# A fused scan, attention and feed-forward kernel: the products of weight matrices move from the attention into the scan

## The reference, cut to what matters

```
x:(64,64,512) float32                                    # 64 sequences, 64 channels, 512 wide
u  = einsum('bct,bcd->bdt', x, weights[cond])            # 64x64 matrix per sequence
x_dbl = einsum('bld,ed->ble', u, x_proj_w)               # delta_r (128), B (16), C (16)
delta = softplus(einsum('blr,dr->bld', delta_r, dt_proj_w) + dt_proj_b)
h_t = exp(delta*A) * h_(t-1) + (delta*u)*B ;  y = sum_n h_t*C  (+ u*D)     # state 16 per channel
x1 = x + y
q,k,v = x1 @ Wq.T, x1 @ Wk.T, x1 @ Wv.T ; q,k = rope(rms(q)), rope(rms(k))
k,v are written into paged blocks (16 tokens a block) ; window 256, softmax, 8 heads on 4 key groups
o  = attention(q, k_all, v_all)                          # (64,64,512)
z  = einsum('bto,do->btd', o, Wo)
s  = einsum('bld,d->bl', z, w_r) ; idx = top_k(s, l/2)   # half of the tokens of a sequence
f  = gelu(z[idx] @ w1 + b1) @ w2 + b2                    # w1 512x2048, w2 2048x512
x_out = x1 + scatter(f, idx)
```

## Time and profile before

| profile of before | |
|---|---|
| median of 3 runs | 1906.06 us |
| the profiled execution | 1905.25 us, span 1903.6 us |
| PE busy | 1671.7 us (88%) |
| DVE busy | 1456.6 us (77%) |
| ACT busy | 1280.2 us (67%) |
| POOL busy | 1268.8 us (67%) |
| chain that ended last | PE 45%, ACT 3%, issue 1%, DMA 1%, DVE 1% |

### The profile page before, as it was taken

One profiled execution on the slowest core, in us unless ns is written; L12 is line 12 of the kernel. 1 busy time (PEld: TensorE's weight loads), 2 busy tenths in 40 slices (PEclk: granted clock), 3 DMA queues, 4 the chain that ended last, 5 costly groups with the idle time before them and its releaser, 6 DMA issues.

```text
span 1903.6 us, 30576 instructions
## 1 busy us (share of the span) xinstructions
PE 1671.7 (88%) x9567; PEld 1154.6 (61%) x9567; DVE 1456.6 (77%) x2572; ACT 1280.2 (67%) x4006; POOL 1268.8 (67%) x1255
## 2 busy tenths in 40 slices
PE   6687878887877787777799899999999999999998
PEld 5665556665665565555355575756657575665765
DVE  8999999999999999999456665655656565565522
ACT  5888888888888888866356664655647465564621
POOL 5789999999999999988777654544545544450000
PEclk9899999999999999888899999999999999999999
DMA  5423323332333223322777434334343443431011
GB/s 207 155 104 147 146 97 124 146 135 109 122 147 147 112 112 142 133 78 73 218 207 217 116 104 124 105 108 130 99 128 103 115 117 110 120 94 60 30 62 45
DMA packets 117745, 230.71 MB, mean 121 GB/s; under 512 B 31365, under 2 KB 70293, under 8 KB 112465
## 3 DMA queue, kind: packets, MB, share of 16 engines
q1 hardware_dynamic: 84496, 163.48, 24.2%
q0 software_dynamic: 33088, 65.28, 12.7%
HBM read 212.09 MB, written 44.70 MB: 135 GB/s over the span
## 4 chain that ended last, share of the span: by engine, by line
PE 45%; ACT 3%; issue 1%; DMA 1%; DVE 1%; POOL 0%; ACTq 0%; DVEq 0%; SPq 0%; POOLq 0%
PE attn_psum L2003 12%; PE attn_psum L2019 12%; PE attn_psum L1933 4%; PE attn_psum L1920 4%; PE attn_psum L1913 4%; PE attn_psum L1960 3%; PE attn_psum L1904 2%; PE attn_psum L2037 2%; PE attn_psum L1894 1%; PE attn_psum L1945 1%; ACT xh L1644 1%; ACT th L1645 1%; ACT prob L1601 0%; DMA kv_at<-kv_scratch,new_now 0%; ACT a_sb L1631 0%
## 5 line engine op out<-in xcount | busy, mean ns | idle before, releaser
L1051 DVE TENSOR_TENSOR_SCAN hid<-scan_psum,hid 128x1024 f32<-128x1024 f32 x256 | 581.1, 2270 | 0.0
L1240 PE MATMUL scan_psum<-ident,hid 128*128 128x128 f32 x2048 | 345.0, 296 | 156.3 <-POOL hid L515 154.8
L1240 PEld LDWEIGHTS scan_psum<-ident,hid 128*128 128x128 f32 x2048 | 263.6, 152 | 301.4 <-POOL hid L515 195.7
L1755 DVE CUSTOM_DVE_ANT_0 prob<-attn_psum,mask 128x336 f32<-128x336 f32 x256 | 119.8, 505 | 267.9 <-PE attn_psum L1913 267.8
L515 POOL TENSOR_TENSOR hid<-hid,kv_at 128x1024 f32<-128x1024 f32 x128 | 306.4, 2407 | 25.7 <-DVE hid L1051 24.7
L515 POOL TENSOR_TENSOR hid<-hid,bc 128x1024 f32<-128x1024 f32 x128 | 306.3, 2406 | 22.7 <-DVE hid L1051 22.3
L1607 ACT COPY p_t<-attn_psum 112x384 f32<-112x384 f32 x256 | 122.8, 488 | 273.5 <-PE attn_psum L1920 273.5
L2019 PE MATMUL attn_psum<-w,ffn_hid 128*128 128x512 f32 x512 | 238.5, 595 | 4.9 <-DVE y_sb L1820 4.9
L1533 POOL DMA_INDIRECT kv_at<-kv_scratch,new_now x189 | 201.0, 1063 | 61.2 <-issue 57.3
L2003 PE MATMUL attn_psum<-xs_in,w 128*128 128x256 f32 x1024 | 232.4, 381 | 7.6 <-ACT xs_in L1613 6.6
L674 ACT ACTIVATE scan_psum<-kv_at,neg_a 128x252 f32<-128x252 f32 x512 | 210.9, 460 | 14.9 <-DVE hid L1051 13.3
(11 more groups left out here) (232 smaller groups left out, 3081.9 us busy)
## 6 DMA issues: line engine op xcount, KB each, us to landing
bc<-bc_scratch SPq DMA_DIRECT2D x16, 2048.0 KB, 7.9
kv_at<-bc_scratch SPq DMA_DIRECT2D x15, 2048.0 KB, 7.6
q_scratch<-qg SPq DMA_DIRECT2D x32, 260.0 KB, 2.0
early<-q_scratch SPq DMA_DIRECT2D x32, 260.0 KB
x_pair<-in_x_pairs SPq DMA_DIRECT2D x32, 256.0 KB, 2.7
kv_scratch<-kvg SPq DMA_DIRECT2D x32, 256.0 KB, 2.0
a_scratch<-a_sb SPq DMA_DIRECT2D x32, 256.0 KB, 3.4
w_o<-x_scratch SPq DMA_DIRECT2D x32, 256.0 KB, 3.4
```

What stands on the lines that cost most here:

```text
L1051: nc.vector.tensor_tensor_scan(states, decay[k % 2], states, 0.0, ALU.mult, ALU.add).then_inc(dve_h, 1)
L1240: mm = nc.tensor.matmul(yc[g], hid[:, e % RING, i, P * g:P * g + P], ident[:], start=False, stop=(k % 4 == 3 and i == 3), is_transpose=Tru ...
```

## The change

Every product of weights is now made within the scan. In quarter s SP loads 128 columns of `w_o` (256 KB), and in every fourth quarter 256 columns of `w1` (512 KB); PE makes half a product of 128 x 512, so 128 x 256, as 4 matrix multiplications in slots 20 to 23, in the unused half of the PSUM bank in which x1 is turned; ACT copies the half out at the start of the next quarter (`take_product`), ahead of the first `take_x1`; SP stores it to a scratch array in HBM. The 32 quarters make the 32 halves. Quarters 1 to 4 also make 128 entries of the router row each (`route`, at the start of chunk 3, in the other such bank), and ACT copies them at chunk 4 (`take_route`), with the second `take_x1` behind them; that one stood ahead of `take_x` and of the softplus. The attention loads the finished `w1'` from the scratch array, its first 128 rows at the start and the others in pairs 1 to 3, and `w2` in pairs 3 to 6; it makes no product. The index columns are no longer copied: the gathers read `idx_old` and `idx_new` themselves. The two products and their copies at the end of the scan block are gone, too.

```
+        f_wo, f_w1 = sb("f_wo", [P, NCH, P]), sb("f_w1", [P, NCH, SUB])
+        f_out, r_out, w_r = sb("f_out", [P, SUB]), sb("r_out", [P, P]), sb("w_r", [P, NCH])
...
+        def folds(n):
+
+            return n + min(n, NROUTE)
+
+        def routed(n):
+
+            return 1 <= n <= NROUTE
...
+            def load_products(s):
+
+                if s:
+                    sp.wait_ge(pe_fold, folds(s - 1) + 1)
+                sp.dma_start(f_wo[:], A["w_o"][:, :, P * (s % NCH):P * (s % NCH) + P]).then_inc(ld_wo, 16)
+                if s % NCH == 0:
+                    sp.dma_start(f_w1[:], A["w1"][:, :, SUB * (s // NCH):SUB * (s // NCH) + SUB]).then_inc(ld_fw, 16)
+
+            def store_products(s):
+
+                if routed(s):
+                    sp.wait_ge(act_fold, folds(s))
+                    sp.dma_start(S["w_or"][:, P * (s % NCH):P * (s % NCH) + P], r_out[0:1, :]).then_inc(st_w, 16)
+                sp.wait_ge(act_fold, folds(s) + 1)
+                sp.dma_start(S["w1"][:, s % NCH, SUB * (s // NCH):SUB * (s // NCH) + SUB], f_out[:]).then_inc(st_w, 16)
+
             def quarter(t, h, q, parts):
                 s = 4 * t + q
+                if parts.scan:
+                    load_products(s)
+                if parts.after_scan:
+                    store_products(s - 1)
...
-                if t == NT - 1 and q == 2:
-                    sp.wait_ge(pool_hc, 8 * (4 * NT - 2))
-                    sp.wait_ge(dve_dbu, 8 * (4 * NT - 2))
-                    for dst, src in zip(early_weights(kv_at), (A["w_o"], A["w1"][:, :, 0:D])):
-                        sp.dma_start(dst, src).then_inc(s_weights, 16)
...
-                if c == 0:
-                    for now, idx in ((old_now, idx_old), (new_now, idx_new)):
-                        pool.tensor_copy(now[b][:], idx[:, :, b:b + 1].rearrange("p c o -> p (c o)")
-                                         ).then_inc(now_ok, 1)
-                    pool.wait_ge(now_ok, 2 * (b + 1))
+                if n == 0:
+                    pool.wait_ge(idx_ok, 2)
                 pool.indirect_dma_start(kv_tile(kv_at, b)[:, c, :], None, A["kv_rows"],
-                                        bass.IndirectOffsetOnAxis(ap=old_now[b][:, c:c + 1], axis=0)
+                                        bass.IndirectOffsetOnAxis(ap=idx_old[:, c, b:b + 1], axis=0)
...
+                def take_product(n):
+
+                    act.wait_ge(pe_fold, folds(n) + 1)
+                    wait(act, st_w, 16 * folds(n))
+                    nc.scalar.copy(f_out[:], y[0][:, SUB:2 * SUB]).then_inc(act_fold, 1)
+
+                def take_route(n):
+
+                    act.wait_ge(pe_fold, folds(n))
+                    wait(act, st_w, 16 * (folds(n - 1) + 1))
+                    nc.scalar.copy(r_out[0:1, :], y[1][0:1, SUB:SUB + P]).then_inc(act_fold, 1)
...
-                    if k in (0, 7 if t == NT else 4) and parts.after_scan:
-                        take_x1(*((t, q - 1) if q else (t - 1, 3)), 1 if k else 0)
+                    if k == 0 and parts.after_scan:
+                        take_product(s - 1)
+                        take_x1(*((t, q - 1) if q else (t - 1, 3)), 0)
...
+                    if k == (7 if t == NT else 4) and parts.after_scan:
+                        if routed(s):
+                            take_route(s)
+                        take_x1(*((t, q - 1) if q else (t - 1, 3)), 1)
...
-                for c in range(NEARLY):
-                    act.wait_ge(pe_last, len(LAST) + c + 1)
-                    nc.scalar.copy(early_weights(kv_at)[2][:, c, :], y[c]).then_inc(act_lc, 1)
...
-                    e_wo, e_w1, _ = early_weights(kv_at)
-                    pe.wait_ge(s_weights, 48)
-                    for c in range(NEARLY):
-                        for j in range(NCH):
-                            mm = nc.tensor.matmul(y[c], e_wo[:, j, P * c:P * c + P], e_w1[:, j, :],
-                                                  start=(j == 0), stop=(j == NCH - 1))
-                        mm.then_inc(pe_last, 1)
+
+                def product(k):
+
+                    if k == 0:
+                        pe.wait_ge(ld_wo, 16 * (s + 1))
+                        pe.wait_ge(ld_fw, 16 * (s // NCH + 1))
+                    mm = nc.tensor.matmul(y[0][:, SUB:2 * SUB], f_wo[:, k, :], f_w1[:, k, :], start=False,
+                                          stop=(k == NCH - 1), skip_group_check=True)
+                    if k == NCH - 1:
+                        mm.then_inc(pe_fold, 1)
+
+                def route():
+
+                    pe.wait_ge(ld_wo, 16 * (s + 1))
+                    for k in range(NCH):
+                        mm = nc.tensor.matmul(y[1][:, SUB:SUB + P], w_r[:, k:k + 1].to_broadcast([P, P]), f_wo[:, k, :],
+                                              start=False, stop=(k == NCH - 1), skip_group_check=True)
+                    mm.then_inc(pe_fold, 1)
...
+                    if k == 3 and routed(s):
+                        route()
...
+                        if parts.scan and 20 <= slot < 24:
+                            product(slot - 20)
...
-                sp.dma_start(w1_in[n % 2], A["w1"][:, :, D * n:D * n + D]).then_inc(ld_w1[n % 2], 16)
+                sp.dma_start(w1[:, n, :], S["w1"][:, n, :]).then_inc(ld_w1, 16)
...
+                if isinstance(m, int) and 1 <= m < NCH + 3:
+
+                    n, c = NF // NCH, m - 3
                     sp.wait_ge(pe_sc, 8 * m + 2)
-                    if m + 1 < NCH:
-                        load_w1(m + 1)
-                    sp.dma_start(W["w2"][:, n * c:n * c + n, :], A["w2"][:, n * c:n * c + n, :]).then_inc(s_w, 16)
+                    if m < NCH:
+                        load_w1(m)
+                    if c >= 0:
+                        sp.dma_start(W["w2"][:, n * c:n * c + n, :], A["w2"][:, n * c:n * c + n, :]).then_inc(s_w, 16)
...
-            sp.dma_start(w_r[:], A["w_r"]).then_inc(s_wo, 16)
-            sp.dma_start(w_o[:], A["w_o"]).then_inc(s_wo, 16)
-            load_w1(0)
...
-            load_w1(1)
+            sp.dma_start(w_or[:], S["w_or"][0].partition_broadcast(P)).then_inc(s_late, 16)
+            load_w1(0)
...
-                if b == 6:
-                    pool.wait_ge(early_half_ok, 1)
-                pool.tensor_copy(old_now[s][:], idx_old[:, :, bass.ds(b, 1)].rearrange("p c o -> p (c o)")
-                                 ).then_inc(now_ok, 1)
-                pool.tensor_copy(new_now[s][:], idx_new[:, :, bass.ds(b, 1)].rearrange("p c o -> p (c o)")
-                                 ).then_inc(now_ok, 1)
-                wait(pool, now_ok, 2 * (b + 1))
                 for c in range(NKC):
                     pool.indirect_dma_start(kv[s][:, c, :], None, A["kv_rows"],
-                                            bass.IndirectOffsetOnAxis(ap=old_now[s][:, c:c + 1], axis=0)
+                                            bass.IndirectOffsetOnAxis(ap=idx_old[:, c, b:b + 1], axis=0)
                                             ).then_inc(ld_old[s], 16)
...
-            def take_fold(at):
-                n = ORDER[at]
-                act.wait_ge(pe_fold, at + 1)
-                b, c = (n - 1) // NCH, (n - 1) % NCH
-                nc.scalar.copy(w1[:, c, D * b:D * b + D] if n else w_or[:], fold_bank).then_inc(act_fold, 1)
-
...
-            def fold(at):
-
-                n = ORDER[at]
-                if n == 0:
-                    pe.wait_ge(s_wo, 32)
-                else:
-                    b, c = (n - 1) // NCH, (n - 1) % NCH
-                    pe.wait_ge(ld_w1[b % 2], 16 * (b // 2 + 1))
-                    pe.wait_ge(act_fold, at)
-                for k in range(NCH):
-                    left = w_o[:, k, P * c:P * c + P] if n else w_r[:, k:k + 1].to_broadcast([P, P])
-                    right = w1_in[b % 2][:, k, :] if n else w_o[:, k, :]
-                    mm = nc.tensor.matmul(fold_bank, left, right, start=(k == 0), stop=(k == NCH - 1))
-                mm.then_inc(pe_fold, 1)
-
...
-                        pe.wait_ge(act_fold, NFOLD)
-                        pe.wait_ge(early_half_ok, 1)
+                        pe.wait_ge(ld_w1, 16 * NCH)
```

More of the change, by code:

```diff
@@ L41 @@
 NKV2 = 1
-NEARLY = 2
+NHALF = 4 * D // SUB
+NROUTE = D // P
 NWS = 6
@@ L86, in early_tiles @@
             [x.rearrange("p (a f) -> p a f", a=2) for x in (rope_0, rope_1)])
-def early_weights(kv_at):
-    w_o, w1, out = (kv_at[:, a:z] for a, z in ((6144, 8192), (8192, 10240), (10240, 10240 + 512 * NEARLY)))
-    return [x.rearrange("p (c n) -> p c n", n=D) for x in (w_o, w1, out)]
 def scan_block(nc, A, S, W):
@@ L115, in scan_block @@
         ident, kv_at, early = W["ident"], W["kv_at"], W["early"]
-        old_now, new_now = W["now"]
-        a_const, now_ok, ld_old, ld_q, ld_kv = (W[n] for n in ("a_const", "now_ok", "ld_old", "ld_q", "ld_kv"))
+        a_const, ld_old, ld_q, ld_kv = (W[n] for n in ("a_const", "ld_old", "ld_q", "ld_kv"))
         diag_d = sb("diag_d", [P, NCH, P])
@@ L418, in _ @@
```

(23 more changed lines are left out.)

31 lines of the change are left out of this document (9 added, 22 removed).

## The result

The changed kernel takes 1920.81 us, median of 6 runs (1916.82 to 1927.90); the kernel before takes 1906.07 (1904.85 to 1907.44) beside it. The ratio is 1.0082, interval 1.0069 to 1.0094: slower by 0.8%, where 1896.5 was predicted. The profiled execution took 1918.95 us, with a span of 1917.2, 13.6 more than before.

A forecast was written before the change was run, and what follows sets the result against it. DVE was taken to bound the scan and POOL's gathers to be second to PE in the attention; +3.4 - 0.9 - 7.5 - 6.2 + 2.5 = -8.7 us against 1905.25 gave 1896.5 us, range 1886 to 1906.

The forecast's parts named there:

- part 1: Scan, half a product per quarter: PE's 1.8 us is covered, ACT's copy waits 0 to 0.2 us, cost 0.
- The prediction's own sign of being wrong: Scan: the forecast is wrong if DVE's idle time there is over 7 us.
- The prediction's bound for the copies: Scan, ACT's copies of half products: cost taken as 0, at most 32 x 0.36 = 11.5 us.
- The router term: Scan, quarters 1 to 4: ACT waits for PE's router piece and DVE stalls, +3.4 us, bounds 0 and 6.4.
- The half products: Scan, all quarters: PE's multiplications and ACT's copies of half products cost 0, bounds 0 and 11.5 us.
- The seam: Between scan and attention: without two products and their copies, -0.9 us, bounds 0 and -1.1.
- POOL's chain: Attention: without index copies, first gather to the other half's gather takes 124.0 us against 131.5, -7.5 us.
- the turn: Attention, gather's issue to PE's turn: PE's lateness through the products goes, -6.2 us, bounds 0 and -6.2.
- The rival with 1856: Attention: PE paces the stage all the same and all removed PE time returns, 49.2 us, 1856; chance 0.05.
- The clock: PE coming back from waiting: one more stretch at half clock, +2.5 us, bounds 0 and 3.8.
- the price that the prediction worked out by it alone: Attention, whole stage at half clock: PE's remaining 80 us would take 160, no gain at all, 1905.
- the scan stalls, slower: Scan: ACT's added wait and copy, or PE's lateness, cost 0.8 us in 27 quarters, 21.6 us, 1918; chance 0.10.

The follow-up runs named there:

- e1_own_count: The changed kernel with the router pieces' stores counted on a semaphore of their own, so ACT's half-product copy no longer waits for them: 1901.38 us, ratio 0.9971 to before.
- e2_no_router: The changed kernel without the router pieces in the scan (no multiplications, copies or stores for them): 1892.47 us, ratio 0.9931 to before.
- e4_own_early: e1_own_count with PE making the router piece one chunk sooner, at the start of chunk 2 in place of 3: 1895.73 us, ratio 0.9948 to before.
- e12: e3 with the router piece one chunk sooner, so e4_own_early without the half products, their copies, loads and stores: 1895.86 us.
- e3: The changed kernel with the router pieces but without the half products; the feed-forward part uses unmultiplied w1: 1900.74 us.
- e6_router_late: e1_own_count with the router pieces in quarters 12 to 15 in place of 1 to 4, at the same chunk: 1905.03 us, ratio 0.9992 to before.
- e11: e4_own_early with the gathers of the first feed-forward tile's two halves two groups of six gathers sooner in POOL's order: 1880.67 us, ratio 0.9865 to before.

## Why the prediction was wrong, step by step

**The step that failed** is in part 1: "It waits for PE's fourth part in slot 23", and for SP, "nothing in the scan waits for the queue long, 0". The copy has a second wait, in the code shown, on a count that includes the router store of its own quarter; and that store is queued on SP behind a load that waits for PE's product. The wait can't be over until PE has finished, SP has issued one or two loads and the store, and the store has landed, 3.1 to 5.6 us, 16.0 in the four quarters, where "0 to 0.2" was taken. Without it the median is 19.4 us lower (the changed kernel against e1_own_count), and DVE's idle time 10.7 in place of 22.4. The prediction's own sign of being wrong, over 7 us of idle time in the scan, showed it. The prediction's bound for the copies, 32 x 0.36, was a price for the instruction and not for its waits.

**The router term** had the right mechanism and the wrong size: +3.4, with a bound of 6.4, against 8.9 (e1_own_count against e2_no_router). PE's piece made ACT wait 7.2 to 8.3 us in four quarters, close to the 2.2 a quarter that was worked out for the fourth. What was wrong is the 0.6 for the other three: margins of ACT in the kernel before were taken for margins after, though a late piece pushes later copies too (the q copy's wait, 5.5 us from 55 to 225 in the kernel before, is 9.5 in e1_own_count and back at 5.8 and 5.2 in e2_no_router and e4_own_early). That even the fourth quarter's 1.6 was right by itself is not shown.

**The half products** were priced right, at 0 (e2_no_router, and e12 against e4). PE's idle time covered them; only beside a late router piece is that open, as said at e3.

**The seam** gave 0.1 of 0.9. POOL's gather after it stands behind 2.09 us that end by its own queue, as the 2.13 us in the row of before, and the copy that ended at 934.04 lay within them; I read past that figure. That this wait hid the gain is a reading, not shown: in e1_own_count and e6_router_late the gather follows at 0.30 us, without it. From the last scan to the first gather the experiments have 31.5 (e6_router_late) to 35.1 us (e4_own_early), so that a term of 0.9 can't be told from scatter.

**POOL's chain** gave 4.8 of 7.5, and the turn 4.1 of 6.2. In e2_no_router the chain is 127.2 us long and the turn follows the issue by 3.4, so 4.4 and 6.7: the first term was too large by some 3 us, since the gaps were worked out with no wait for a landed DMA (L1550 waited 3.4 us for such in the changed kernel and 5.4 in e2_no_router, against 1.8 before), and the second was right. In the changed kernel it fell short because the gather took 5.9 us to land, in place of 3.9; a load of `w2` of 1 MB, which the change had moved to these pairs, was under way then, but no run shows that it was the cause. That PE is idle in the stage and waits for POOL's gathers was right: PE waited 23.2 us for keys and values, against 2.9 before, and 18.1 for the rows, and of the products' 51.7 us only 9.0 came back. The rival with 1856 was rightly rare.

**The clock** was granted at 0.81 in the stage, against 0.96, and the time from the turn to the end grew by 1.8 us where 2.5 was taken. In the first 11.5 us of it the granted clock was 0.73, with PE busy for 11.2, where it was 1.00 behind the turn of the kernel before; that can be the 1.8 us, but no run separates it. The rule cited from the Trainium skill (TensorE: Matmul & The Clock Gate, Part 1: The HAM clock gate) fits the clock's fall, but not the price that the prediction worked out by it alone, no gain at all in the stage: the stage was 9.0 us shorter. That a slower PE cost little there because it waited for DMAs anyway is argued, not shown.

**The rival "the scan stalls, slower"** named the right side and, at 1918, nearly the time, with a chance of 0.10; its mechanism was not what happened. It spread 0.8 us over 27 quarters by ACT's or PE's own work; the loss is in quarters 1 to 5, the most of it behind a landing DMA. Coming near its 1918 was luck.

**Left open:** the changed kernel's runs are 11 us apart and e11's 10 us, where the kernel before has 2.6. No run separates the cause.

## What to carry to other kernels

When a change adds a wait on a counted semaphore, write down everything that the count includes and where each increment is issued: a shared counter makes a copy wait for stores that have nothing to do with its buffer, and the queue of the issuing engine can put such a store behind a wait for the very work that is being copied. In a stage whose pacing engine has no slack, price a new instruction by its last-arriving wait, and by how near it stands to the pacing engine's next instruction, not by its duration. And when one engine's work is taken out of a stage, look at the order of the next one's: once the products had moved and the scan was repaired (e4_own_early, about 10 us below the kernel before), two gathers moved forward in POOL's list were worth another 15.1 (e11_all_rows_two). What they would be worth in the kernel before was not run; there PE turned the rows 6.2 us after they had landed.

## What the runs showed of the hardware

A store of 512 bytes issued at 152.91 (0.47 us) released its waiter at 156.38, 3.5 us later, and the three others like it after 2.2 to 2.4 us: a small DMA is no cheap handshake here. And indirect DMAs that read their indices from a column with a stride are as fast as those that read a packed copy: 1040 and 976 ns before, 1044 and 978 ns over the same 93 gathers of the changed kernel.
